# A transformer layer on one core: the feed-forward block's rotation split by PSUM bank, its output projection one step later

## What is computed

```python
h = shift_token(x)                       # right half of each row comes from the row before
q, k, v = split(h @ wqkv)                # 8 heads of 64
q = l2norm(q) * qs;  k = l2norm(k) * ksc
q, k = rotary_xpos(q, k)                 # x*cos*scale + rotate_half(x)*sin*scale
o = local_attention(q, k, v)             # windows of 64 rows, keys of this window and the last
x = x + o @ wo
h = shift_token(x)
h = layernorm(h) * lg + lb
a, g = split(h @ w1 + b1);  x = x + (a * gelu(g)) @ w2 + b2
```

## Time and profile before

| | us |
|---|---|
| median of 3 runs | 5035.81 (5032.77 to 5036.17) |
| the profiled execution | 5039.37, with a span of 5037.7 in the trace |
| PE busy in the span | 3958.2 (79%) |
| DVE busy | 2871.0 (57%) |
| ACT busy | 2620.8 (52%) |
| POOL busy | 1703.7 (34%) |

### The profile page before, as it was taken

The page is one execution under the profiler, slowest core; times in us unless marked ns, Lnnn a source line. Parts: engine busy times, 40 slices in busy tenths (PEclk is TensorE's granted clock), DMA queues, the critical chain, the costliest instruction groups (busy, mean ns, idle before and its releaser), DMA issues.

```text
span 5037.7 us, 101534 instructions
## 1 busy us (share of the span) xinstructions
PE 3958.2 (79%) x31924; PEld 2425.0 (48%) x31924; DVE 2871.0 (57%) x5889; ACT 2620.8 (52%) x6422; POOL 1703.7 (34%) x1415
## 2 busy tenths in 40 slices
PE   2999999996688888744666664999999917888886
PEld 1555555553455555522222222777777715555554
DVE  2555555555566676543444443666666656767664
ACT  1555555553566666423333332666666605666664
POOL 0000000000777777523222221111111128777773
PEclk9999999998899999865555555999999959999998
DMA  3222222221101101017999999777777611111111
GB/s 122 78 79 82 78 79 78 84 77 45 44 22 23 24 23 23 16 66 287 382 381 378 381 379 370 260 243 273 242 275 243 227 34 26 23 23 23 23 24 28
DMA packets 373723, 701.02 MB, mean 139 GB/s; under 512 B 53220, under 2 KB 160056, under 8 KB 373608
## 3 DMA queue, kind: packets, MB, share of 16 engines
q1 hardware_dynamic: 329576, 565.25, 32.8%
q0 software_dynamic: 44032, 134.30, 7.3%
HBM read 336.53 MB, written 314.64 MB: 129 GB/s over the span
## 4 chain that ended last, share of the span: by engine, by line
PE 60%; DMA 13%; DVE 7%; issue 7%; POOL 5%; ACT 3%; SPq 1%; DVEq 1%; POOLq 0%; ACTq 0%
DMA rel_k<-b_stage_k 12%; PE ps L332 5%; PE ps L1452 5%; PE ps L340 5%; PE ps L351 5%; PE ps L1461 5%; PE ps L862 4%; PE ps L1443 3%; PE ps L821 3%; PE ps L1472 3%; PE ps L882 2%; PE ps L836 2%; PE ps L847 2%; POOL f_rn L759 2%; PE ps L1344 2%
## 5 line engine op out<-in xcount | busy, mean ns | idle before, releaser
L1368 DVE COPY b_stage_k<-ps 128x640 f32<-128x640 f32 (+2 forms) x512 | 359.3, 722 | 471.1 <-DMA rel_k<-b_stage_k 412.3
L430 ACT ACTIVATE a_p<-a_s,a_min 128x512 f32<-128x512 f32 x512 | 367.1, 718 | 469.6 <-DVE a_min L474 469.6
L1365 ACT ACTIVATE b_stage_q<-ps 128x640 f32<-128x640 f32 (+2 forms) x512 | 316.4, 624 | 506.8 <-PE ps L1347 390.2
L474 DVE CUSTOM_DVE_ANT_0 a_s<-ps,a_table 128x512 f32<-128x512 f32 x512 | 333.5, 689 | 374.4 <-PE ps L332 371.8
L1526 ACT ACTIVATE c_p<-c_s,c_min 128x512 f32<-128x512 f32 x512 | 371.0, 725 | 291.9 <-PE ps L1461 179.8
L1344 PE MATMUL ps<-b_e,b_st_k 48*128 48x512 bf16 (+1 forms) x512 | 305.9, 597 | 263.8 <-DVE b_stage_k L1368 263.8
L1561 DVE CUSTOM_DVE_ANT_0 c_s<-ps,c_rq 128x512 f32<-128x512 f32 x512 | 353.2, 690 | 202.5 <-PE ps L1452 189.8
L188 POOL COPY y<-ln_rows 128x512 f32 x32 | 19.9, 621 | 1305.2 <-DVE ln_rows L180 1305.2
L757 POOL TENSOR_TENSOR f_rot<-f_rc,f_rs 128x1024 f32<-128x1024 f32 x128 | 302.9, 2367 | 354.3 <-DVE f_rs L1017 354.0
L942 ACT ACTIVATE f_p<-f_s,f_min 128x128 f32<-128x128 f32 x1024 | 397.6, 392 | 39.6 <-DVE f_min L1005 35.6
L759 POOL TENSOR_TENSOR f_rn<-f_ss,f_power 128x16 f32<-128x16 f32 x128 | 373.8, 2920 | 14.3 <-DVE f_ss L1026 0.4
(11 more groups left out here) (171 smaller groups left out, 9374.7 us busy)
## 6 DMA issues: line engine op xcount, KB each, us to landing
rel_q<-b_stage_q SPq DMA_DIRECT2D x64, 1280.0 KB, 7.7
rel_k<-b_stage_k SPq DMA_DIRECT2D x64, 1280.0 KB, 7.7
c_rq<-rel_q SPq DMA_DIRECT2D x64, 1024.0 KB, 7.3
c_rk<-rel_k POOLq DMA_DIRECT2D x64, 1024.0 KB, 11.8
a_table<-skew_bias SPq DMA_DIRECT2D x64, 896.0 KB, 4.6
f_vb<-f_v SPq DMA_DIRECT2D x256, 128.0 KB, 2.3
rel_k<-b_stage_k SPq DMA_DIRECT2D x32, 1024.0 KB, 9.4
rel_q<-b_stage_q SPq DMA_DIRECT2D x32, 1024.0 KB, 5.3
```

The lines of the kernel that those rows point to most:

```text
L430: nc.scalar.activation(a_p[:, lt % 2, h, :], a_s[:, lt % 2, h, :], ACT.Exp, bias=a_min[:, lt % 2, h:h + 1], scale=-1.0, accum_out=a_sum[:, ...
L1368: moves_b1(dve, 1, lambda out, src: nc.vector.tensor_copy(out, src))
```

## The change

- The square (ACT) and the three multiplications of the rotation (DVE) are each done once for the q bank and once for the k bank: two squares of 128x512 and six multiplications (two of 128x512, four of 128x256). The projection, the squares, the multiplications and `transpose_qk` wait for each other bank by bank.
- `join_heads` and the addition to y work on a tile `d`, four behind `a`. `join_heads` stands right after the v projection and writes MIXED; the addition stands on DVE right after L1055. `mix_values` waits until that addition has freed MIXED.
- In step 3, DVE's `mask_and_min` stands behind `turn_heads`, the copy, the addition and `sum_squares`; ACT's order is not changed.
- DVE's `statistics` stands behind the reciprocal. The DMAs that shift rows into `f_h` are issued in step 3 instead of step 2, behind that step's `f_vb` DMAs; POOL's copy of the left half of `f_h` goes to the end of its step 3.

```diff
 # SP
-        def step(m, a, b, s2, c, ln, mlp, nxt):
+        def step(m, a, b, s2, c, d, ln, mlp, nxt):
             if a is not None:
                 hold(sp, f_v_moved, upto(a.g))
                 hold(sp, f_pv, upto(a.g - 3))
                 sp.dma_start(f_vb[WINDOW:P, m, :], f_v[0:WINDOW, m, :]).then_inc(f_vb_loaded[m], 16)
                 sp.dma_start(f_vb[0:WINDOW, (m + 1) % LT, :], f_v[WINDOW:P, m, :]).then_inc(f_vb_loaded[m], 16)
-            if m == 2 and ln is not None:
+            if m == 3 and ln is not None:
                 half = slice(DIM // 2, DIM)
-                hold(sp, f_x_mid, upto(c.g))
+                hold(sp, f_x_mid, upto(d.g))
                 hold(sp, f_hn_ready, upto_b(ln.g - 1, LT))
 # POOL: the copy into f_h
-            if m == 3 and ln is not None:
-                hold(pool, f_x_mid, upto(ln.g * LT + 3))
...
+            if m == 3 and ln is not None:
+                hold(pool, f_x_mid, upto(ln.g * LT + 3))
 # PE
-            mm(ps[:, QK, :], h, f_wqkv[:, a.layer, 0:INNER], start=True, stop=True)
+            mm(ps[:, QK, :], h, f_wqkv[:, a.layer, 0:INNER], start=True, stop=True).then_inc(f_qk_full, 1)
             mm(ps[:, QK + 1, :], h, f_wqkv[:, a.layer, INNER:2 * INNER], start=True, stop=True).then_inc(f_qk_full, 1)
...
-            pe.wait_ge(f_oT_moved, upto(c.g - 1))
+            pe.wait_ge(f_x_mid, upto(c.g - 1))
...
+                if a is not None:
+                    pe.wait_ge(f_squared, upto(a.g - 1, 2) + k + 1)
+                    pe.wait_ge(f_turned, upto(a.g - 1, 6) + 3 * k + 3)
...
-        def join_heads(a, c):
+        def join_heads(m, d, mlp):
+            if m == 0 and mlp is not None:
+                pe.wait_ge(f_y_done, upto_b(mlp.g - 1))
+            if m == 1 and mlp is not None:
+                pe.wait_ge(f_hnT_moved, upto_b(mlp.g))
+            if m == 2 and mlp is not None:
+                pe.wait_ge(f_gelued, upto_b(mlp.g, 3))
+            if m == 3 and mlp is not None:
+                pe.wait_ge(f_hid_ready, upto_b(mlp.g, 3))
+            pe.wait_ge(f_oT_moved, upto(d.g))
...
 # ACT
-                nc.scalar.activation(f_sq[:, :], ps[:, QK:QK + 2, :].rearrange("p b n -> p (b n)"),
-                                     ACT.Square).then_inc(f_squared, 1)
+                for k in range(2):
+                    act.wait_ge(f_qk_full, upto(a.g - 1, 2) + k + 1)
+                    nc.scalar.activation(f_sq[:, k * INNER:(k + 1) * INNER], ps[:, QK + k, :],
+                                         ACT.Square).then_inc(f_squared, 1)
 # DVE
-            if s2 is not None:
+            if s2 is not None and m < 3:
                 mask_and_min(s2)
...
+            if d is not None:
+                dve.wait_ge(f_out_full, upto(d.g))
+                tt(y[:, d.t, :], y[:, d.t, :], ps[:, MIXED, 0:DIM], ALU.add).then_inc(f_x_mid, 1)
             if a is not None:
                 sum_squares(a)
+            if s2 is not None and m == 3:
+                mask_and_min(s2)
             if m == 0 and mlp is not None:
                 normalize(mlp)
-            if m == 3 and ln is not None:
-                statistics(ln)
...
-            if c is not None:
-                dve.wait_ge(f_out_full, upto(c.g))
-                tt(y[:, c.t, :], y[:, c.t, :], ps[:, V_BANK, 0:DIM], ALU.add).then_inc(f_x_mid, 1)
+            if m == 3 and ln is not None:
+                statistics(ln)
```

More of the change, by code:

```diff
@@ L654, in body @@
             for m in range(LT):
-                step(m, rows(0, m), rows(1, m), rows(2, m), rows(3, m), whole(-1), whole(-2), whole(1))
+                step(m, rows(0, m), rows(1, m), rows(2, m), rows(3, m), rows(4, m), whole(-1), whole(-2), whole(1))
         body(0, 0)
@@ L826, in transpose_qk @@
         def transpose_qk(a, b):
[L827 to L832, removed]
-            pe.wait_ge(f_normed, upto(b.g))
-            for k, full in enumerate((f_qT_full, f_kT_full)):
+            pe.wait_ge(f_normed, upto(b.g))
+            for k, (full, moved) in enumerate(((f_qT_full, f_qT_moved), (f_kT_full, f_kT_moved))):
+                if a is not None:
+                    pe.wait_ge(f_squared, upto(a.g - 1, 2) + k + 1)
+                    pe.wait_ge(f_turned, upto(a.g - 1, 6) + 3 * k + 3)
+                else:
+                    pe.wait_ge(moved, upto(b.g - 1))
                 for i in range(PAIRS_F):
@@ L838, in transpose_qk, with mixed_free, turn_normed @@
                 last.then_inc(full, 1)
-        def join_heads(a, c):
[L841 to L845, removed]
+        def join_heads(m, d, mlp):
[8 more added lines that the diff above has]
+            pe.wait_ge(f_oT_moved, upto(d.g))
             for i in range(PAIRS_F):
-                last = mm(ps[:, V_BANK, 0:DIM], f_oT[:, i * P:(i + 1) * P], f_wo[:, c.layer, i, :],
+                last = mm(ps[:, MIXED, 0:DIM], f_oT[:, i * P:(i + 1) * P], f_wo[:, d.layer, i, :],
                           start=(i == 0), stop=(i == PAIRS_F - 1))
             last.then_inc(f_out_full, 1)
-        def turn_normed(c, mlp):
-            if c is None:
-                pe.wait_ge(f_y_done, upto_b(mlp.g - 1))
+        def mixed_free(c, d):
+            if c is not None:
+                pe.wait_ge(f_oT_moved, upto(c.g))
+            elif d is not None:
+                pe.wait_ge(f_x_mid, upto(d.g))
+        def turn_normed(c, d, mlp):
+            mixed_free(c, d)
+            pe.wait_ge(f_y_done, upto_b(mlp.g - 1))
             pe.wait_ge(f_hn_ready, upto_b(mlp.g, LT))
@@ L891, in step @@
                 project_v(a, h)
+            if d is not None:
+                join_heads(m, d, mlp)
             if c is not None:
@@ L896, in step @@
             if c is not None:
-                mix_values(m, c, mlp)
+                mix_values(c)
             if m == 1 and mlp is not None:
@@ L1010, in turn_heads @@
             dve.wait_ge(f_rotated, upto(a.g - 1))
[L1011 to L1018, removed]
+            for k in range(2):
+                heads = ps[:, QK + k, :].rearrange("p (h d) -> p h d", d=DF)
+                rc = f_rc[:, k * INNER:(k + 1) * INNER].rearrange("p (h d) -> p h d", d=DF)
+                rs = f_rs[:, k * INNER:(k + 1) * INNER].rearrange("p (h d) -> p h d", d=DF)
+                dve.wait_ge(f_squared, upto(a.g - 1, 2) + k + 1)
+                tt(rc, heads, cs[:, 0, k, :].unsqueeze(1).broadcast_to([P, HF, DF]), ALU.mult).then_inc(f_turned, 1)
+                for h in range(2):
+                    to, src = slice(h * 32, h * 32 + 32), slice((1 - h) * 32, (1 - h) * 32 + 32)
+                    tt(rs[:, :, to], heads[:, :, src],
+                       cs[:, 1, k, to].unsqueeze(1).broadcast_to([P, HF, 32]), ALU.mult).then_inc(f_turned, 1)
         def sum_squares(a):
```

36 lines of the change are left out of this document (15 added, 21 removed).

## The result

The changed kernel takes 5336.18 us, median of 4 runs (5331.05 to 5344.57), against 5035.77 for the kernel before: a ratio of 1.060, 95% interval 1.0581 to 1.0618, so 6% slower. The forecast was 5330. The profiled execution spans 5334.3 us.

A forecast was written before the change was run, and what follows sets the result against it. No engine is full; PE's waits set the period. Batch 25.3 + 23.65 + 11.93 = 60.9 against 51.5 us, +9.4; over 30 batches +282, ends 12, together +294 on 5039.4: forecast 5330, range 5275 to 5415.

The forecast's parts named there:

- step 3 to the mixing: From the start of step 3's q projection to PE's mixing, held by ACT's late f_pT: 11.7 us, before 8.4.
- mixing to the `f_vb` DMA: Step 3, from the mixing's start on PE to the f_vb DMA on SP: 1.9 us, at the slow clock.
- from there to the shift: Step 3 on SP's queue, from the f_vb DMA to the shift DMA behind it: 1.2 us with the two holds.
- landing: From the shift DMA's issue to statistics on DVE: 10.5 us as before, at most 2.3 more if queued behind f_vb transfers.
- `statistics` to `transpose_probs` in step 1: From the start of statistics through DVE's mask and rotation and POOL's chain to PE's transpose_probs in step 1: 16.8 us.
- to step 2: From PE's transpose_probs in step 1 to the start of step 2's q projection: 6.82 us, 7.82 less 1.0 for join_heads.
- step 2: From step 2's q projection to the next step 3's: 11.93 us instead of 12.93, the mixing held by ACT as before.
- low clock: PE's 1.2 GHz level, expected at step 3's mixing after 6.2 us idle; full clock would save 0.7 us a batch.
- signs named in advance: Expected: no idle before step 3's transposes, some 6 us before its mixing, some 8 in step 0, statistics waiting over 8.
- the ends: First batches and drain of both calls: 3 us each, 12 in all, range 0 to 24.
- a price of 0.2 us: DVE's rotation in six pieces takes 2.5 us instead of 2.3, so 0.2 us more.
- rival 2: Faster: each step hangs on the QK banks' release, placed at step 3's transpose_qk; 5.4 us a batch, about 4874; chance 0.03.

The follow-up runs named there:

- mask alone: Kernel before with only step 3's mask_and_min moved behind sum_squares: 5239.38 us (ratio 1.0406), where 5160 was expected.
- shift alone: Kernel before with only the shift DMAs issued in step 3 behind the f_vb DMAs and statistics behind reciprocal and addition: 5317.94 us (1.0562), expected 5280.
- split alone: Kernel before with only squares, rotation and transpose_qk done bank by bank: 5084.05 us (1.0095), where 4990 was expected.

## Why the prediction was right

The forecast was 5330, the median 5336. Leg by leg, us per batch, forecast and measured: step 3 to the mixing 11.7 and 1547.93 - 1536.47 = 11.5; mixing to the `f_vb` DMA 1.9 and 2.1; from there to the shift 1.2 and 1.6, the one term that was clearly too small; landing 10.5 and 10.54, so nothing queued behind `f_vb`; `statistics` to `transpose_probs` in step 1 16.8 and 1578.73 - 1562.14 = 16.6; to step 2 6.8 and 7.0; step 2 11.9 and 11.93. Sum 60.9 and 61.2. The low clock at the mixing was as expected (L815 0.45 for four instead of 0.32 at full clock). The signs named in advance came: no wait in front of the transposes in step 3, 6.08 us before the mixing for some 6 expected, and 6.99 in step 0 for some 8. That last wait stands in another place than forecast, at the output projection for the MLP's addition and not at the transposes for the rotation. It changes nothing in the sum, which runs over DVE and POOL there, and PE still waits 1.70 for POOL in step 1.

The number was luckier than the legs. The forecast took one batch for all 30. These are the starts of step 3 of the first and the last batch of each call:

| | call 1 | us | call 2 | us |
|---|---|---|---|---|
| before | 1306.29 to 2073.32 | 767.0 | 4180.48 to 4951.54 | 771.1 |
| after | 1304.18 to 2209.17 | 905.0 | 4325.65 to 5232.48 | 906.8 |

That is 273.7 more in 30 distances, 9.1 each, not the 9.4 of the forecast (282) or the 9.7 of the batches shown: 7 of 26 batches of the kernel before take 54 to 55 us and not 51.5, since PE has the low clock in step 0 too. The trace grew by 5334.3 - 5037.7 = 296.6, so 22.9 lie in the ends, nearly twice the 12 allowed. The term of the batches was 8 too large and that of the ends 11 too small; the two cancel.

The mechanism is shown, not only consistent: undoing the shift's place gives back 237 us, undoing the mask 175, spreading the transfer 218; and in the kernel before the place alone costs 282 and the late mask alone 203. They don't add up. With both undone 7.25 us of the shift's wait and 51 us of the loss are left, for the lag of four steps holds the transfer by itself.

What else was right by luck of the case: I gave the split a price of 0.2 us in the sum (its six pieces take 1540.69 - 1538.16 = 2.5 us, as estimated), and in rival 2 a large gain. Alone it costs 48 us, through the granted clock, which I had priced in step 3 only. In the changed kernel this is not seen, where the low clock lies in steps 3 and 0 (0.81 and 0.82) and steps 1 and 2 have 1.00; that the long idle times fix it there is likely, but no run tests it. The two expectations that missed by more than 30 us (mask alone 79, shift alone 38) and the one that missed in sign (split alone, 94) all had PE's granted clock too high in a step. In the first two the waits were right up to the first work after the idle time: the mixing at 12.55 for 12.6, `statistics` at 22.2 (1469.34 to 1491.56) for 22.5.

## What to carry to other kernels

When a transfer is moved down a queue, price what the queue's head waits for, not the issue itself: ten microseconds of landing that a step had hidden became part of the loop as soon as the DMA stood behind one that waits for this step's matmuls. A wait that "costs nothing now", as `statistics` had, is the first place to look at. And one batch is not the average of them: read the period from the first to the last before multiplying by 30. An operation put later on one engine is paid by whoever stands behind its consumer in another engine's fixed order, here `f_pT` behind four exponentials.

## What the runs showed of the hardware

- The pair of DMAs over 127 partitions and one took 10.5 us from issue to use, with a DMA share of 0.06 in flight; the same bytes over 112, 15 and one took 3.85, with a share of 0.33. Behind the 127 partitions the issue of the one-row DMA took 6.9 us, behind the 15 it took 0.77.
- How long PE idles doesn't settle its clock by itself. In the kernel before, PE idled 2.35 us before the transposes of one step 0 and fell to the 1.2 GHz level (1.74 us for eight matmuls); in the next batch it idled 2.34 us and kept 2.4 GHz (1.09). In the kernel with the late mask alone the low level came after the same idle time in 25 of 26 batches, in the kernel before in 7.
- In the split alone the one wait before the transposes became two shorter ones (1.84 and 0.60 us in step 3, 1.19 and 0.60 in step 0). With it went a granted clock of 0.88 in steps 1 and 2, which had had 1.00. With one wait again, and nothing else changed, they had 1.00.
